# Four spills with a semaphore each and two order tables for the filling of a pipelined delta-rule attention

## The reference

```
qkvz = layernorm(x) @ W_qkvz           # 16 key heads, 32 value heads of 128
q, k, v = silu(causal_conv4(q, k, v))  # a filter of 4 taps along the tokens of a sequence
q = l2norm(q) * 128 ** -0.5;  k = l2norm(k)
g = -exp(A_log) * softplus(a + dt_bias);  beta = sigmoid(b)
for each token:                        # the delta rule, one state of 128 x 128 for each value head
    state = state * exp(g)
    state = state + k * ((v - k @ state) * beta)
    out = q @ state
y = rmsnorm(out) * norm_weight * silu(z) @ W_out
```

## Time and profile before

| | us |
|---|---|
| median of 3 runs | 2986.46 |
| lowest and highest | 2980.61, 2987.47 |
| the profiled execution | 2988.33 |
| its span, first to last instruction | 2986.1 |
| busy in the span: TensorE, VectorE, ScalarE, GpSimd | 2701.9, 1930.2, 1397.8, 678.0 |

### The profile page before, as it was taken

The page is one execution under the profiler, slowest core; times in us unless marked ns, Lnnn a source line. Parts: engine busy times, 40 slices in busy tenths (PEclk is TensorE's granted clock), DMA queues, the critical chain, the costliest instruction groups (busy, mean ns, idle before and its releaser), DMA issues. The chain is left out here.

```text
span 2986.1 us, 58338 instructions
## 1 busy us (share of the span) xinstructions
PE 2701.9 (90%) x19346; PEld 1997.4 (67%) x19347; DVE 1930.2 (65%) x3648; ACT 1397.8 (47%) x4441; POOL 678.0 (23%) x938
## 2 busy tenths in 40 slices
PE   4899995556999999999999999999999995799996
PEld 4566663333677777777777777777777774566664
DVE  5122222588999999999999999999987544322221
ACT  0111111333667667666666766766765551111111
POOL 0222221222222221221222222222221101122221
PEclk7999997777999999999999999999999996799998
DMA  4133312244645545545555545545543313132322
GB/s 160 45 79 102 96 28 53 73 140 146 199 150 188 161 148 185 163 148 183 168 145 180 172 147 174 176 148 169 177 144 95 104 54 119 31 96 65 100 61 46
DMA packets 378124, 374.74 MB, mean 125 GB/s; under 512 B 213076, under 2 KB 293460, under 8 KB 377876
## 3 DMA queue, kind: packets, MB, share of 16 engines
q1 hardware_dynamic: 362900, 351.05, 37.3%
q0 software_dynamic: 14976, 20.46, 4.1%
HBM read 234.83 MB, written 138.67 MB: 125 GB/s over the span
## 5 line engine op out<-in xcount | busy, mean ns | idle before, releaser
L533 PE MATMUL f_ps_up<-f_wbuf,f_xgT 128*128 x1248 | 500.3, 544 | 5.1 <-issue 3.2
L628 DVE TENSOR_TENSOR f_h<-f_h,f_ps_up 128x448 f32<-128x448 f32 x156 | 96.9, 621 | 472.2 <-ACT f_h L602 472.2
L602 ACT ACTIVATE f_h<-f_ps_up 128x448 f32<-128x448 f32 x156 | 85.0, 545 | 635.9 <-PE f_ps_up L533 635.9
L533 PEld LDWEIGHTS f_ps_up<-f_wbuf,f_xgT 128*128 128x128 f32 x1248 | 231.6, 192 | 189.7 <-issue 185.1
L1270 PE MATMUL at_bank<-xnT,at_w_qk 128*128 128x512 f32 x512 | 273.2, 662 | 58.9 <-DVE at_qk L1597 55.5
L1597 DVE SCALAR_TENSOR_TENSOR at_qk<-at_bank,at_taps_qk,at_qk 128x510 f32<-128x510 f32 (+2 forms) x384 | 281.9, 744 | 64.9 <-ACT at_qk L1468 55.5
L1597 DVE SCALAR_TENSOR_TENSOR at_vT<-at_bank,at_taps_v,at_vT 128x510 f32<-128x510 f32 (+2 forms) x384 | 280.4, 744 | 36.5 <-ACT at_vT L1475 27.5
L1846 POOL TENSOR_SCALAR at_small<-at_small 128x4 f32<-128x4 f32 x64 | 17.3, 270 | 1154.6 <-ACT at_squares L1502 1154.6
L500 POOL DMA_INDIRECT sums<-f_y,f_row_of x78 | 123.9, 1589 | 582.7 <-DVE f_y L639 582.7
L555 PE MATMUL f_ps_y<-f_wbuf,f_hT 128*128 x1092 | 248.8, 379 | 1.6 <-DVE f_hT L632 1.6
L1295 PE MATMUL at_bank<-at_w_vz,xnT 128*128 128x256 f32 x1024 | 243.6, 381 | 7.0 <-DVE at_vT L1597 6.9
(11 more groups left out here) (232 smaller groups left out, 5657.4 us busy)
## 6 DMA issues: line engine op xcount, KB each, us to landing
f_wbuf<-in_L_ffn_w_dram SPq DMA_DIRECT2D x48, 896.0 KB, 6.8
at_steps_e<-steps_kept SPq DMA_DIRECT2D x64, 512.0 KB, 6.7
pt_kept<-at_pt_made SPq DMA_DIRECT2D x64, 512.0 KB, 2.7
mt_kept<-at_mt_made SPq DMA_DIRECT2D x64, 512.0 KB, 4.1
at_mt<-mt_kept SPq DMA_DIRECT2D x64, 512.0 KB, 4.0
at_pt<-pt_kept SPq DMA_DIRECT2D x64, 512.0 KB, 4.5
qk_kept<-at_qk SPq DMA_DIRECT2D x64, 256.0 KB, 2.7
ks_kept<-at_ks_made SPq DMA_DIRECT2D x64, 256.0 KB, 2.7
```

Of the source, the lines that this page charges most:

```text
L533: last = te.matmul(ps_up[hf][w][:, 0:MH], xgT[b][:, k, :], wbuf[:, bass.ds(off + (w * WSIZE + k * M + hf * MH), MH)], start=(k == 0), stop ...
L628: v.tensor_tensor(part, part, ps_up[hf][1][:, 0:MH], ALU.mult).then_inc(h_ready, 1)
```

## The change

The step `spill` becomes four steps, `spill_qk`, `spill_ks`, `spill_pt` and `spill_mt`, with a pair of semaphores each, and each has a place of its own in SP's tables. Each waiter waits for the spill that it needs alone. The filling gets two tables for each engine: `FRONT_` for iterations -12 to -7 and a new `FILL_` for -6 to -2. The steady and drain tables keep their order, with the four spills side by side where `spill` was. `seen` counts what `walk` has issued up to there, in place of the formula. `proj_qk` gets one more wait, for `v_free` of its bank. `steps_e` and `decay` stay single buffers.

```diff
-    "spill": 11,
+    "spill_qk": 11, "spill_ks": 11, "spill_pt": 11, "spill_mt": 11,
...
 SP_ORDER = (("load_wo",), ("load_c",), ("load_d",), ("load_steps",), ("load_t",), ("blocks_in",), ("store_up",),
-            ("spill",), ("store_low",), ("load_qk",), ("load_vz",))
+            ("spill_qk",), ("spill_ks",), ("spill_pt",), ("spill_mt",), ("store_low",), ("load_qk",), ("load_vz",))
...
+def phase_of(i):
+
+    if i < -STAGE["blocks"]:
+        return "front"
+    if i < -STAGE["proj_v"]:
+        return "fill"
+    return "steady" if i < UNITS + FIRST else "drain"
...
-        def seen(u, at, of):
-
-            return min(max(idx(u) - STAGE[at[0]] + STAGE[of[0]] + (BEFORE[of] < BEFORE[at]), 0), UNITS)
+        issued = Counter()
+
+        def seen(of):
+
+            return issued[of]
...
-            filling, steady, draining = orders
+            issued.clear()
             for i in range(FIRST, UNITS + AFTER):
-                for name, *args in filling if i < -STAGE["proj_v"] else steady if i < UNITS + FIRST else draining:
+                for name, *args in orders[phase_of(i)]:
                     u = shift((i // BP, i % BP), STAGE[name])
                     if 0 <= idx(u) < UNITS:
                         steps[name](u, *args)
+                        issued[(name, *args)] += 1
...
-                def spill(u):
-                    done = s["spilled"][two(u)]
+                def spill_qk(u):
                     sp.wait_ge(s["qk_ready"], 2 * idx(u) + 2)
                     late = qk[two(u)][:].rearrange("p a (b c m) -> p (a b) c m", b=2, c=2)[:, :, 1, :]
-                    sp.dma_start(unit_rows(qk_kept, u), late).then_inc(done, 16)
+                    sp.dma_start(unit_rows(qk_kept, u), late).then_inc(s["qk_spilled"][two(u)], 16)
+
+                def spill_ks(u):
                     sp.wait_ge(s["k_ready"], idx(u) + 1)
...
                     for k in range(2):
-                        sp.wait_ge(s["spilled"][k], SPILL * (2 * u[0] + 2))
+                        sp.wait_ge(s["mt_spilled"][k], 16 * (2 * u[0] + 2))
...
                 def load_c(u):
...
-                    sp.wait_ge(s["spilled"][two(u)], SPILL * of_two(u))
+                    sp.wait_ge(s["mt_spilled"][two(u)], 16 * of_two(u))
...
                 def load_d(u):
...
-                    sp.wait_ge(s["spilled"][two(u)], SPILL * of_two(u))
+                    for kept in ("pt_spilled", "ks_spilled", "qk_spilled"):
+                        sp.wait_ge(s[kept][two(u)], 16 * of_two(u))
...
                 def proj_qk(u, ct):
...
                     at_least(pe, s["qk_free"], 2 * idx(u) - 1 + ct)
-                    at_least(pe, s["z_free"], 2 * seen(u, me, ("z", ct)) - 1 + ct)
-                    at_least(pe, s["added"], 2 * seen(u, me, ("project", ct)) - 1 + ct)
+                    at_least(pe, s["v_free"], 2 * seen(("proj_v", 2 + ct)) - 1 + ct)
+                    at_least(pe, s["z_free"], 2 * seen(("z", ct)) - 1 + ct)
+                    at_least(pe, s["added"], 2 * seen(("project", ct)) - 1 + ct)
...
                 def conv_qk(u, ct):
...
-                    at_least(act, s["spilled"][two(u)], SPILL * (of_two(u) - 1))
+                    at_least(act, s["qk_spilled"][two(u)], 16 * (of_two(u) - 1))
...
                 def ks_(u):
...
-                    at_least(act, s["spilled"][1 - two(u)], SPILL * of_two(shift(u, -1)))
+                    at_least(act, s["ks_spilled"][1 - two(u)], 16 * of_two(shift(u, -1)))
...
                 def mix(u, of):
...
-                    at_least(dve, s["spilled"][1 - two(u)], SPILL * of_two(shift(u, -1)))
+                    at_least(dve, s["pt_spilled" if of else "mt_spilled"][1 - two(u)], 16 * of_two(shift(u, -1)))
```

More of the change, by code:

```diff
@@ L1 @@
+from collections import Counter
 from contextlib import ExitStack
@@ L921 @@
 FIRST, AFTER = -max(STAGE.values()), -min(STAGE.values())
[L923 to L936, removed]
@@ L937 @@
-FILL_POOL_ORDER = (("norm_scale",), ("scales",), ("diag",), ("low",))
+FRONT_SP_ORDER = (("load_steps",), ("spill_ks",), ("store_low",), ("load_c",), ("load_wo",), ("store_up",),
+                  ("load_t",), ("load_vz",), ("load_qk",), ("load_d",), ("spill_qk",), ("blocks_in",), ("spill_mt",),
+                  ("spill_pt",))
+FRONT_PE_ORDER = (("project", 0), ("y_turn", 0), ("z", 0), ("proj_qk", 0), ("proj_v", 2), ("turn", 1), ("state",),
+                  ("turns", 0), ("inv_last",), ("inv_x", 64), ("inv_x", 32), ("turn", 0), ("output", 0),
+                  ("project", 1), ("y_turn", 1), ("proj_qk", 1), ("proj_v", 3), ("output", 1), ("z", 1),
+                  ("products", 0), ("solve", 0), ("on_state", 0), ("turns", 1), ("solve", 1), ("on_state", 1),
+                  ("products", 1), ("inv_n",))
@@ new lines @@
+FRONT_ACT_ORDER = (("z_gate", 0), ("turn_copies", 0), ("turn", 1), ("turn", 0), ("conv_qk", 0), ("y_copy", 0),
+                   ("inv_last",), ("conv_qk", 1), ("ks",), ("weigh", 0), ("gate_qk", 0), ("from_state",),
+                   ("y_copy", 1), ("z_gate", 1), ("conv_v", 2), ("inv_n",), ("copy_state",), ("norm",), ("gate_v", 2),
+                   ("gate_qk", 1), ("conv_v", 3), ("gate_v", 3), ("turn_copies", 1), ("weigh", 1), ("lift",))
+FRONT_DVE_ORDER = (("shape",), ("blocks", 0), ("conv_qk", 0), ("conv_qk", 1), ("scan",), ("blocks", 1), ("conv_v", 2),
+                   ("mix", 0), ("blocks", 2), ("add", 0), ("inv_x", 32), ("add", 1), ("inv_x", 64), ("join",),
+                   ("blocks", 3), ("conv_v", 3), ("mix", 1), ("from_state",))
@@ new lines @@
+FRONT_POOL_ORDER = (("scales",), ("norm_scale",), ("diag",), ("low",))
+FILL_SP_ORDER = (("load_steps",), ("blocks_in",), ("load_vz",), ("load_wo",), ("load_qk",), ("load_c",), ("load_t",),
+                 ("spill_ks",), ("store_up",), ("spill_qk",), ("load_d",), ("store_low",), ("spill_mt",),
+                 ("spill_pt",))
+FILL_PE_ORDER = (("y_turn", 0), ("proj_v", 2), ("y_turn", 1), ("proj_qk", 0), ("state",), ("solve", 0), ("turn", 1),
+                 ("z", 0), ("turn", 0), ("on_state", 0), ("z", 1), ("inv_x", 32), ("solve", 1), ("products", 0),
+                 ("inv_last",), ("products", 1), ("on_state", 1), ("inv_n",), ("output", 0), ("turns", 0),
+                 ("inv_x", 64), ("project", 0), ("output", 1), ("project", 1), ("turns", 1), ("proj_v", 3),
+                 ("proj_qk", 1))
@@ new lines @@
+FILL_ACT_ORDER = (("norm",), ("gate_v", 2), ("turn", 1), ("lift",), ("gate_v", 3), ("from_state",), ("turn", 0),
+                  ("conv_v", 2), ("y_copy", 0), ("conv_qk", 0), ("conv_v", 3), ("turn_copies", 0), ("z_gate", 0),
+                  ("ks",), ("conv_qk", 1), ("inv_last",), ("inv_n",), ("weigh", 0), ("turn_copies", 1),
+                  ("copy_state",), ("weigh", 1), ("y_copy", 1), ("gate_qk", 0), ("z_gate", 1), ("gate_qk", 1))
+FILL_DVE_ORDER = (("add", 0), ("conv_v", 2), ("blocks", 0), ("blocks", 1), ("conv_qk", 0), ("inv_x", 64),
+                  ("blocks", 2), ("conv_qk", 1), ("scan",), ("blocks", 3), ("mix", 0), ("add", 1), ("join",),
+                  ("shape",), ("conv_v", 3), ("from_state",), ("mix", 1), ("inv_x", 32))
@@ L1241, in bank1_read @@
                 def bank1_read(u, me):
[L1243 to L1247, removed]
+                    at_least(pe, s["s_ready"], seen(("state",)))
+                    at_least(pe, s["k_ready"], seen(("turn", 1)))
```

73 lines of the change are left out of this document (43 added, 30 removed).

## The result

The changed kernel takes 2953.63 us (median of four runs, 2949.91 to 2958.01); the kernel before, timed beside it, 2986.75 (2980.61 to 2987.47). The ratio is 0.9894, 95% interval 0.9875 to 0.9913: faster by 1.1%, 33 us. The forecast was 2955.5. The profiled execution took 2953.89 us with a span of 2951.7 (before 2988.33 and 2986.1).

What follows compares the result with a forecast made beforehand. TensorE was taken to bound the steady stage, a chain of waits through mt's landing the filling. Terms 2.0 + 18.5 + 3.9 + 7.3 - 0.5 = 31.2 off 2986.5 gave 2955.5 us, own range 2948 to 2962.

Steps and rivals of the forecast that it cites:

- First unit, 2.0: Iteration -11: TensorE's turns stand ahead of proj_qk 1 and the products, so scan 0 starts 2.0 us earlier.
- Front, 18.5: Units 1 to 4: turns of 10.1 us (9.2 to 11.7) in place of 14.6; gain 18.5 us, bounds 12 to 22.
- three rings: Front's remaining wait cycles, longest sets the turn: VectorE's work 9.2 us, projection's bank 10.0, single steps_e buffer 10.0.
- projection's ring: Front: conv_qk 0's filter, proj_qk 0, turn, squares, copy, filter again; 10.0 us, or 8.1 with the projection half as long.
- Iterations -6 to -3, 3.9: VectorE's waits before conv_qk (2.80, 0.66, 0.41) go, as copies no longer wait for mt; gain 3.9 us, 0 to 4.
- Iteration -2, 7.3: store_up leaves as w_up is done, so the second group's blocks stop waiting; gain 7.3 us, bounds 3 to 7.3.
- TensorE's wait, -0.5: proj_qk's added v_free wait before 104 steady-stage projections: cost taken as 0.5 us, between 0 and 5.8.
- Steps load sets a long turn: Rival, front: steps_e landings of 6.5 make turns 12.2 us; gain 22.5, time 2964; chance 0.12.
- Front doesn't shorten: Rival: another link holds the front's turn near 14.6 us; 13 us of gain remain, 2973; chance 0.08.
- store stays late: Rival: SP is held elsewhere at iteration -3 and the 7.3 us isn't gained; 2963 us; chance 0.06.
- Hidden: Rival: first steady iterations wait for transfers that don't start earlier, eating the lead; 2980 to 2987 us; chance 0.05.
- Slower: Rival: the 104 added waits cost a TensorE without slack; at 0.35 us each, 36 us, time 2992; chance 0.03.

Runs made afterwards that it cites:

- the semaphores alone: The changed kernel with both filling tables put back to the old order, only the four spill semaphores kept; 2973.50 us, ratio 0.9955 to the kernel before.
- the two moves: Kernel before plus the four semaphores, old filling order with turns directly behind proj_qk 0 and store_up behind spill_ks; 2959.06 us, ratio 0.9912.
- store late: The changed kernel with store_up moved from behind spill_ks to behind spill_pt in the filling; 2958.04 us, ratio 0.9908 to the kernel before.
- old filling, store early: The changed kernel with its new front, but iterations -6 to -1 in the old order with store_up moved behind spill_ks; 2954.64 us, ratio 0.9892.
- semaphores and TensorE's orders: The changed kernel with the queues of SP, ScalarE, VectorE and POOL in the old filling order; 2960.49 us, ratio 0.9915 to the kernel before.

## Why the prediction was right, step by step

- **What bounds.** A chain of waits in the filling, with mt's landing in it: right. The sum, 31.2, stands against 32.9 in the stretch and 33.1 by the medians. That it comes so close is in part luck: the terms missed by +0.8 us (front), -1.2 (iterations -6 to -3), +1.0 (-2) and +0.7 (scan 9 to 12, for which nothing was forecast and no cause is shown).
- **First unit, 2.0:** 1.93. The first square comes 1.9 us earlier relative to the start.
- **Front, 18.5:** 19.33. Of the three rings named the single steps_e buffer was the one that bound; its landing, taken as 4.8, took 4.76, 4.60, 4.74 and 4.72. With the load sent earlier the turn fell to the 9.2 named as VectorE's own work (9.37 measured). The first turn, forecast 0.4 shorter than the others, took 9.86, since it hung on that load too. The projection's ring was priced at 10.0 with the clock of the earlier trace rows; that clock did not come: in the front 1.00 was granted and proj_qk took 1.96 us, so the prediction's other price for this ring, 8.1, is the one that applies. This misjudgement cost nothing, as the steps load was longer than either.
- **The reason was incomplete in one point.** "With the mt landing out of the chain, three cycles are left" is true of both halves together. With the semaphores alone a fourth is left, through the products that stand ahead of the turns. The prediction gave the turns' new place 2.0 us in the first unit; it is worth 1.9 more in each turn (12.9 with the semaphores alone, 11.0 with the two moves, of which the store's plays no part in the front).
- **qk's spill as the tightest new wait:** right. ScalarE waited for it twice in the changed kernel, 1.1 us in all, behind the longer steps load; with that load early it cost 1.2 us once.
- **Iterations -6 to -3, 3.9:** 2.67. The waits of the earlier trace rows went. Two losses were not in the prediction. VectorE went on with the blocks at 615.29 after 0.92 us of waiting for their load: the front was shortened by more than the load behind its spills. And two instructions of the blocks took 1.6 us more than their equals, as POOL's diag ran beside them; in these iterations the kernel before lost 0.9 in this way (below).
- **Iteration -2, 7.3:** 8.27. The 7.29 of the earlier trace rows went whole, and with the store late a wait of 6.27 came back. The rest is one small instruction of the blocks, which took 1.06 us beside POOL's diag in the kernel before and 0.16 in the changed one (below). Nothing in the change aims at this 0.9; it is luck.
- **TensorE's wait, -0.5:** -0.08 in the steady stage. The bound of 5.8 taken from L1270 against L1283 did not measure this wait: without it the difference of 14 ns stays (606 against 592), and eight more of it leave the mean at 602 and show as idle time instead.
- **The rivals.** "Steps load sets a long turn" needed landings of 6.5; 4.7 came. "Front doesn't shorten" and "store stays late" are what the kernels without one part show (turns of 12.9, a wait of 6.27), not what the change does. "Hidden": scan 12's lead of 32.06 us is still 31.98 at scan 63. "Slower": decides from 0.30 us a wait; even eight more at one place show only 0.35 us together.

## What to carry to other kernels

A semaphore that stands for several transfers makes every reader wait for the last of them; splitting it pays only as far as the next ring below allows, so list the rings of the steady turn with their lengths and remove the two longest together. A store that a later step reads back belongs in the queue where its data is ready, not behind the transfers that it has nothing to do with. In a bound stage look for what a single buffer's reload stands behind: moving one load ahead of two spills, and two other loads out of the way, took 3.9 us off the stretch here without a further buffer.

## What was unexpected of the hardware

- The shorter front had the full clock. Before, 0.76 was granted at 34.03 us busy in 58; after, 1.00 at 28.48 in 40. In the next stretch it was 0.73 at 39.46 in 63. The projection's price of 3.75 us, taken at 0.50 in the kernel before, was 1.96 in the shortened front: a price holds for the clock at which it was taken.
- The same loads in the same queue order landed 4.6 to 4.8 us after their issue in one profile and up to 6.0 in another (old filling, store early, whose front has the same tables). A turn that hangs on a landing can vary by as much.
- In the kernel before, one of eight equal VectorE instructions of the blocks, 128x8 elements, took 1.06 us where the others took 0.15. It began 0.09 us after POOL's diag and ended 0.02 us after it. The changed kernel has the same in iteration -6. The eight instructions and diag, first before, then after:

```profile
709.44 1.65 DVE L1670 TENSOR_TENSOR at_terms<-at_w_up,at_up 128x8 f32<-128x8 f32 x8
709.63 1.13 POOL L1821 TENSOR_SCALAR_AFFINE_SELECT at_decay<-at_t_b 128x1024 f32<-128x1024 f32 x1
```

```profile
616.50 1.65 DVE L1729 TENSOR_TENSOR at_terms<-at_half_way,at_w_up 128x8 f32<-128x8 f32 x8
...
616.85 1.13 POOL L1867 TENSOR_SCALAR_AFFINE_SELECT at_decay<-at_t_b 128x1024 f32<-128x1024 f32 x1
```

In the twelve profiles, up to 724 us, fifteen of VectorE's two-input instructions of the blocks (those that write at_terms) began inside diag, at least 0.04 us after its start and 0.08 before its end. Each took 0.33 to 0.92 us longer than the shortest of its equals, which is 0.12 to 0.17 us less than what was left of diag. No other took over 0.25 us longer. Behind the waits of 6.27 (store late) and 5.74 (semaphores and TensorE's orders) diag ran at another time, and all eight took 0.71 together. No run moves diag by itself, so that it is the cause rests on these coincidences.
